# The first feed-forward product in seven block products for eight, on one NeuronCore

## The chip, the core and the metric

The kernel runs on one NeuronCore of a Trainium2 chip. The metric is device microseconds of one launch, from the first instruction to the end of the last store. The five engines are TensorE (PE in the profile, its weight loads PEld), VectorE (DVE), ScalarE (ACT), GpSimd (POOL) and SyncE (SP, here the queue that issues nearly all DMAs). Each engine runs its own instructions strictly in the order in which the program wrote them, and waits on semaphores that others raise. So an instruction that waits holds up everything behind it on its engine.

## What is computed

A transformer layer on x of 8 batches of 512 tokens and 512 features: cross attention with 16 heads, then a feed-forward part with a routed low-rank addition. The change is about the second part:

```
def _L0_ffn_ref(x, W1, W2, ln_g, ln_b, router_W, router_b, raw_U, raw_V, gamma):
    r_raw = _layernorm(x_flat, ln_g, ln_b) @ router_W.T + router_b
    r = jnp.clip(r_raw, -TAU, TAU)
    alpha = jax.nn.softplus(r)
    phi, idx = jax.lax.top_k(alpha, TOP_K)
    S_sum = jnp.sum(phi, axis=-1, keepdims=True)
    Z = phi / (S_sum + EPS) * jnp.tanh(S_sum)
    h_lat = jnp.einsum('nd,nkd->nk', x_flat, U_sel)
    dyn = jnp.einsum('nk,nkd->nd', h_lat * Z, V_sel).reshape(B, S, D) * gamma
    static = (jax.nn.gelu(x_flat @ W1.T, approximate=False) @ W2.T).reshape(B, S, D)
    return static + dyn
x = x + _L0_xattn_ref(_layernorm(x, axis=-1), ctx, ctx, mask, bias, ...)
x = x + _L0_ffn_ref(_layernorm(x, axis=-1), ...)
```

W1 is 2048 by 512, W2 is 512 by 2048, the router has 256 rows, and 8 of them are chosen per token.

## The kernel before

Three stages run one after the other, each a function: `project` (to about 290 us: the q, k and v products, and W1 and W2 split and stored for later), `attend` (to 853 us), and `blend` (to the end at 1799 us). The change is nearly all in `blend`.

**Precision.** A product of two float32 matrices is computed as three products of rounded halves (PASSES, high by high, high by low, low by high; type fp32r). The halves come from a copy to the high half and a subtraction for the low half. `project` stores both halves of W1 and W2 in `wf_d`, and `blend` loads them as pieces of 512 KB for each batch again (`load_w1`, `load_w2`, four slots each).

**The feed-forward loop.** A batch is 16 blocks f of 128 hidden features. `up(b, p, f)` makes one block for the batch's 512 tokens: 12 matmuls of 512 columns at L1695 (4 chunks of the inner dimension by 3 passes) that take W1's block as the stationary operand and the normalised tokens `zT` as the moving one. ScalarE applies the gelu (L1574), VectorE casts the high half `g_h` (L1463), GpSimd subtracts for the low half `g_l` (L1281). `down(b, f)` adds the block into the output, 12 matmuls at L1716, and is placed two blocks behind its `up` (LAG = 2). `ps_h` is two PSUM banks that `up` fills in turn.

**The rest of a batch** is spread over the same loop by block number: the output projection of the next batch's attention (`project_out`, 48 matmuls at L1618, blocks 6 and 7), the residual and the statistics on VectorE (`residual`, L1310 and L1313), normalisation and turning of the next tokens (block 8 and 9, L1327, L1612), routing of the next batch (`route`, blocks 10 to 12), softplus on ScalarE (`soften`, L1552 to L1557), choice and weights on VectorE (`choose`, `weigh`, `gains`, L1358 to L1397), then `turn_h` and `latent`. The tokens `zT` are held twice, so that all of this for batch b+1 runs beside batch b. All orders are written out by hand in each engine's `body`; no scheduler moves anything.

## Time and profile before

| | us |
|---|---|
| three runs, median (lowest to highest) | 1801.02 (1800.64 to 1802.78) |
| span of the profiled execution | 1799.0 |
| one batch in steady state (1064.13 to 1181.06) | 116.93 |
| TensorE busy in it | 116.93 |
| VectorE, ScalarE, GpSimd busy in it | 40.46, 24.32, 30.29 |

The profiled execution spans 1799.0 us from its first to its last instruction; the median of the runs is 2.0 us above that, which is what lies around the span and the scatter of the runs together. In a row of the trace's timeline the first number is the start in us from the span's beginning, the second the duration, then engine, line, operation, output and inputs with their shapes, and in brackets the idle time before it and who ended it. A matmul's duration overlaps with its neighbours', so the distance between two starts is what one costs.

### The profile page before, as it was taken

The page shows a single profiled execution, that of the slowest core. Times are in us where ns is not written, and L with a number is a line of the kernel's source. Part 1 is how long each engine was busy: PE and PEld are TensorE (multiplying, and loading weights), DVE is VectorE, ACT ScalarE, POOL GpSimd, SP SyncE. Part 2 cuts the span into 40 slices and gives each one's busy share as a digit, 9 for nine tenths or more (in the row PEclk, how much of TensorE's full clock was granted, in tenths as well). Part 3 has the DMA queues.
Part 4 walks back from the last instruction along what each step waited for, and adds up shares of the span by engine and source line. Part 5 has one row for each costly group of instructions (what it writes and reads, how often), then busy time and mean ns, then how long its engine had stood idle before and what let it go on. Part 6 is the DMA issues. An engine that isn't in the chain of part 4 may idle for free.

```text
span 1799.0 us, 29674 instructions
## 1 busy us (share of the span) xinstructions
PE 1784.4 (99%) x10800; PEld 1335.5 (74%) x10800; DVE 1041.7 (58%) x2438; ACT 813.8 (45%) x1819; POOL 832.9 (46%) x368
## 2 busy tenths in 40 slices
PE   9999999999999999999999999999999999999999
PEld 7888886555555555555788888888888888888887
DVE  7565558999999999998852324333342242332411
ACT  4322226999999999998232113122131131311300
POOL 1212128999999999996221232222312223223222
PEclk9999999999999999999999999999999999999999
DMA  9998999536346335420543645535546355464453
GB/s 327 338 358 291 343 337 363 191 110 221 97 140 202 128 126 203 138 93 19 201 153 116 213 157 175 188 117 189 191 143 226 128 188 170 138 217 154 152 188 128
DMA packets 198160, 339.98 MB, mean 189 GB/s; under 512 B 10625, under 2 KB 52225, under 8 KB 197505
## 3 DMA queue, kind: packets, MB, share of 16 engines
q1 hardware_dynamic: 194464, 324.98, 53.4%
q0 software_dynamic: 3264, 12.58, 1.9%
q8 instruction: 88, 1.44, 0.3%
q10 hardware_dynamic: 288, 0.52, 0.1%
q14 instruction: 56, 0.45, 0.1%
HBM read 268.84 MB, written 69.21 MB: 188 GB/s over the span
## 4 chain that ended last, share of the span: by engine, by line
PE 51%; DVE 1%; POOL 0%; issue 0%; ACT 0%; DVEq 0%; POOLq 0%; ACTq 0%
PE banks L1695 19%; PE banks L1716 19%; PE banks L1618 11%; PE banks L1612 1%; DVE k_x L1310 0%; DVE k_x L1455 0%; DVE n_aT_l L1302 0%; DVE n_zT_l L1302 0%; DVE n_stats L1313 0%; POOL n_rstd L1262 0%; POOL k_x L1256 0%; DVE h_k L1403 0%; POOL n_rs L1271 0%; DVE h_q L1421 0%; PE banks L1681 0%
## 5 line engine op out<-in xcount | busy, mean ns | idle before, releaser
L1281 POOL TENSOR_TENSOR n_g_l<-h_pos,n_g_h 128x512 fp32r<-128x512 f32 x128 | 175.1, 1368 | 601.9 <-DVE n_g_h L1463 601.9
L1716 PE MATMUL banks<-n_w,n_g_h 128*128 128x512 f32 x1024 | 316.7, 391 | 0.0
L1574 ACT ACTIVATE h_pos<-banks 128x512 f32<-128x512 f32 x128 | 75.5, 596 | 512.2 <-PE banks L1695 512.1
L1695 PE MATMUL banks<-n_zT_h,n_w 128*128 128x512 f32 x896 | 297.1, 390 | 0.0
L1463 DVE CAST n_g_h<-h_pos 128x512 fp32r<-128x512 f32 x128 | 54.4, 427 | 378.1 <-ACT h_pos L1574 378.1
L1063 ACT ACTIVATE l_tiles<-l_tiles,l_small 128x512 f32<-128x512 f32 x376 | 267.4, 715 | 0.1
L997 DVE CUSTOM_DVE_ANT_0 l_tiles<-banks,l_tiles 128x512 f32<-128x512 f32 x353 | 224.8, 687 | 25.8 <-PE banks L899 24.6
L910 PEld LDWEIGHTS banks<-ident,l_tiles 128*128 128x128 f32 x1524 | 163.3, 141 | 90.1 <-issue 70.5
L1716 PEld LDWEIGHTS banks<-n_w,n_g_h 128*128 128x128 f32 x1024 | 191.2, 188 | 39.3 <-POOL n_g_l L1281 0.4
L910 PE MATMUL banks<-ident,l_tiles 128*128 128x128 f32 x1524 | 207.5, 279 | 1.0 <-ACT a_pT L1041 0.9
L1716 PE MATMUL banks<-n_w,n_g_l 128*128 128x512 f32 x512 | 199.5, 390 | 0.0
L1695 PEld LDWEIGHTS banks<-n_zT_h,n_w 128*128 128x128 f32 x896 | 168.2, 188 | 34.7
L1695 PE MATMUL banks<-n_zT_l,n_w 128*128 128x512 f32 x448 | 174.4, 389 | 0.0
L1004 DVE COPY a_pT<-banks 128x512 f32<-128x512 f32 x256 | 164.5, 683 | 4.0 <-PE banks L910 3.1
L1041 ACT ACTIVATE a_pT<-banks 128x512 f32<-128x512 f32 x256 | 151.4, 592 | 29.1 <-PE banks L910 24.9
L924 PE MATMUL banks<-a_pT,a_v 128*32 128x256 f32 x2048 | 149.9, 388 | 0.0
L899 PE MATMUL banks<-h_k,h_q 32*128 32x512 f32 x1008 | 143.7, 639 | 2.4 <-PEq L158 0.5
L864 POOL TENSOR_TENSOR l_tiles<-a_pos,l_bias 128x2048 f32<-128x2048 f32 (+1 forms) x32 | 137.2, 4299 | 3.6 <-PE banks L910 3.3
L1716 PEld LDWEIGHTS banks<-n_w,n_g_l 128*128 128x128 f32 x512 | 96.1, 188 | 20.1
L406 POOL TENSOR_TENSOR p_wf_l<-l_pos,p_wf_h 128x2048 fp32r<-128x2048 f32 x8 | 36.9, 4615 | 141.8 <-ACT p_wf_h L562 141.8
L1695 PEld LDWEIGHTS banks<-n_zT_l,n_w 128*128 128x128 f32 x448 | 84.2, 188 | 17.3
L1063 ACT ACTIVATE a_t_s<-a_t_s,l_small 128x512 f32<-128x512 f32 x128 | 91.5, 719 | 0.0
(230 smaller groups left out, 3199.5 us busy)
## 6 DMA issues: line engine op xcount, KB each, us to landing
n_w<-wf_d SPq DMA_DIRECT2D x256, 512.0 KB, 4.2
a_pos<-pos_d SPq DMA_DIRECT2D x16, 1024.0 KB, 5.6
l_bias<-in_bias POOLq DMA_DIRECT2D x9, 1024.0 KB, 8.3
l_tiles<-in_x SPq DMA_DIRECT2D x8, 1024.0 KB, 10.6
l_bias<-in_mask SPq DMA_DIRECT2D x8, 1024.0 KB, 14.2
k_d<-l_tiles SPq DMA_DIRECT2D x8, 1024.0 KB, 12.8
pos_d<-l_bias SPq DMA_DIRECT2D x8, 1024.0 KB, 12.2
v_d<-p_v_s SPq DMA_DIRECT2D x32, 256.0 KB, 7.0
```

The lines of the kernel that those rows point to most:

```text
L864: pool.tensor_tensor(out=t_s[j % NN][:, first:end, :], in0=pos_rows(b, qt, qt + 1).broadcast_to([P, end - first, S]), in1=bias_rows(first, ...
L899: pe.matmul(ps_s[:, i, :], q[rows, b, qt * P:(qt + 1) * P], k[rows, b, :], start=True, stop=True).then_inc(scored, 1)
L910: last = pe.transpose(ps_t[:, BANK[i], kt * P:(kt + 1) * P], t_s[at[1] % NN][:, i, kt * P:(kt + 1) * P], ident[:, :])
L924: last = pe.matmul(ps_o[rows, :], v[:, b, kt, rows], pT[:, h, i, kt, :], start=kt == 0, stop=kt == NT - 1)
L997: dve.tensor_tensor_reduce(t_s[j % NN][:, i:i + 1, :], ps_s[:, i:i + 1, :], added, 1.0, 3.0e38, ALU.add, ALU.min, nmax[:, j % NN, i:i + 1] ...
L1004: dve.tensor_copy(dst, src).then_inc(kept_dve, 1)
L1041: act.activation(dst, src, ACT.Copy).then_inc(kept_act, 1)
L1063: act.activation(t_s[j % NN][:, i, :], t_s[j % NN][:, i, :], ACT.Exp, scale=-1.0, bias=nmax[:, j % NN, i:i + 1], accum_out=total[:, j // 2 ...
L1281: pool.tensor_tensor(out=g_l[:, f % NG, :], in0=g_f[:, f % NG, :], in1=g_h[:, f % NG, :].bitcast(F32), op=ALU.subtract).then_inc(g_low, 1)
L1618: last = pe.matmul(dst, stationary, moving, start=start and n == 0, stop=stop and n == len(passes) - 1)
L1695: last = pe.matmul(ps_h[:, f % 2, :], stationary, moving, start=i == 0, stop=i == len(passes) - 1)
L1716: last = pe.matmul(ps_y[:, t, :], gs[i], w2[:, f % NW, j, :], start=f == 0 and m == 0, stop=f == NF - 1 and m == 2)
```

## The change

The product of W1 and the tokens is cut into two by two blocks: W1 into two halves of its hidden features and two of its inner dimension, the tokens into two halves of the inner dimension and two of the tokens. With sums of blocks on both sides, seven block products give what eight give (the scheme with 7 products and 15 additions). A batch is 8 units, each with the pair of 128-feature blocks f and f + 8. A unit has the products P1, P6, P2, P7, P5, P4 and P3, in this order on TensorE (`product`, L1848). Each is 6 matmuls of 256 columns (2 chunks by 3 passes, L1871), and so a batch has 336 matmuls of 256 columns for 192 of 512 columns. `down` is kept: 12 matmuls of 512 columns per block, now in four pieces `down(j, t)` of 3, spread between the products.

- **The results are put together from PSUM.** ScalarE copies P1 (`c1`, L1739). VectorE adds `u2` = P6 + c1 and `u3` = P7 + c1, then C22 = bank + u3, C21 = bank + c1 and C12 = bank + u2. P2 is added in PSUM to P1, P7 and P4 to P6, and P3 to P5, and a product that lands in a bank waits until the one before was read. The gelu takes three instructions per unit instead of two.
- **The tokens' sums.** `z_copies` take the turned tokens from PSUM, `z_sums` makes four sums on VectorE, `z_highs` and `z_lows` split the blocks, `z_sum_lows` on GpSimd splits the sums. The result `zo` is held once, not twice. Therefore the first unit of a batch (f = 0) has a seam on TensorE: the 8 pieces of `down` that are due, the last two turns and `latent` stand ahead of the new batch's first product.
- **W1's sums** are made in `project` by GpSimd (`weight_sums`), and seven operands per unit are stored in place of W1 and W2. In `blend` 448 loads of 256 KB fetch them into 9 slots.
- **W2** is loaded raw, 128 loads of 256 KB, and split again for each batch: `weight_high` on ScalarE (L1721), `weight_low` on GpSimd (L1356), two of each per unit.
- **The small work is placed anew.** Routing is of the batch itself, in its units 0 and 1; softplus is in unit 2, cut in two (`soften` ahead of the gelus of the unit, `soften_more` behind them), the weights in units 3 and 4, `turn_h` in unit 5, the next batch's `project_out` and `residual` in units 6 and 7. In batch 0 routing comes one unit later. `split(3, ...)` of `vg`, which before stood behind two casts, now stands ahead of the first unit on VectorE.
- Several semaphores are merged into one with a running count.

The core of the diff (removed loops stand in the functions above):

```diff
-    wf_d = nc.dram_tensor("wf_d", (NF, P, 4, D), F32, kind="Internal").ap()
+    wf_d = nc.dram_tensor("wf_d", (NF // 2, P, NP, 2, S // 2), F32, kind="Internal").ap()
...
+            def weight_low(j):
+                pool.wait_ge(w2_high, j + 1)
+                pool.tensor_tensor(out=w2[:, j % NG, 1, :], in0=w2_raw[:, j % 2, :], in1=w2[:, j % NG, 0, :].bitcast(F32),
+                                   op=ALU.subtract).then_inc(w2_low, 1)
...
+                gelu_low(2 * n - 1)
+                if f == UNITS - 1 and more:
+                    roots(b + 1)
+                weight_low(2 * n)
+                gelu_low(2 * n)
+                weight_low(2 * n + 1)
+                if f == 4 and more and b > 0:
+                    add_bo(b + 1, (b + 1) % 2)
...
+            split(3, vg[0][:, :, :], vg[1][:, :, :], lat_vg[:, :, :])
...
+            def behind_u2(b, f):
+                at, m = f - route_at(b), b + 1
+                if at in (0, 1):
+                    logits(b, 2 * at)
+                if f == 1 and b > 0:
+                    evacuate(b - 1, 0)
+                    evacuate(b - 1, 1)
+                if at == 2:
+                    clip(b)
+                    largest(b)
+                if at == 3:
+                    small_part(b)
+                if at == 4:
+                    weigh(b)
+                if f == UNITS - 1 and b < B - 1:
+                    if b > 0:
+                        residual(m, 3)
+                    moments(m)
+
+            def behind_u3(b, f):
+                at, m = f - route_at(b), b + 1
+                if f == 1 and b > 0:
+                    evacuate(b - 1, 2)
+                    evacuate(b - 1, 3)
+                if at in (0, 1):
+                    logits(b, 2 * at + 1)
+                if at == 2:
+                    choose(b)
+                if at == 3:
+                    large_part(b)
+                if at == 5:
+                    h_lows(b)
+                    if b < B - 1 and b > 0:
+                        att_low(m, (0, 1))
+                if f == 6 and b < B - 1 and b > 0:
+                    residual(m, 0)
+                if f == UNITS - 1 and b < B - 1:
+                    normalise(m)
+
+            def behind_c12(b, f):
+                at, m = f - route_at(b), b + 1
+                if at == 2:
+                    chosen(b)
+                if at == 3:
+                    alpha(b)
+                if at == 4:
+                    gains(b)
+                if at == 5 and b < B - 1 and b > 0:
+                    att_low(m, (2, 3))
+                if f == 6 and b < B - 1 and b > 0:
+                    residual(m, 1)
+                    residual(m, 2)
...
+                if f == 0 and b > 0:
+                    z_sums(b, 0)
+                    z_lows(b, 0)
+                    z_sums(b, 1)
+                    z_lows(b, 1)
+                dve.wait_ge(made, NP * n + P6 + 1)
+                dve.wait_ge(c1_done, n + 1)
+                dve.tensor_tensor(out=u2, in0=y_bank, in1=c1, op=ALU.add).then_inc(posted, 1)
+                gelu_high(2 * n - 1)
+                behind_u2(b, f)
+                dve.wait_ge(made, NP * n + P7 + 1)
+                dve.tensor_tensor(out=u3, in0=y_bank, in1=c1, op=ALU.add).then_inc(posted, 1)
+                behind_u3(b, f)
+                dve.wait_ge(made, NP * n + P5 + 1)
+                dve.wait_ge(posted, NPOST * n + U3)
+                need(dve, g_low, 2 * n - NG + 1)
+                dve.tensor_tensor(out=row_1[:, HALF:S], in0=x_bank, in1=u3, op=ALU.add).then_inc(posted, 1)
+                dve.wait_ge(made, NP * n + P4 + 1)
+                dve.tensor_tensor(out=row_1[:, 0:HALF], in0=y_bank, in1=c1, op=ALU.add).then_inc(posted, 1)
+                dve.wait_ge(made, NP * n + P3 + 1)
+                need(dve, g_low, 2 * n + 1 - NG + 1)
+                dve.tensor_tensor(out=row_0[:, HALF:S], in0=x_bank, in1=u2, op=ALU.add).then_inc(posted, 1)
+                gelu_high(2 * n)
+                behind_c12(b, f)
...
+                act.wait_ge(made, NP * n + P1 + 1)
+                act.activation(c1, ps_h[:, n % 2, 0:HALF], ACT.Copy).then_inc(c1_done, 1)
+                if at in (0, 1):
+                    keep_lat(b, 2 * at)
+                act.wait_ge(made, NP * n + P2 + 1)
+                need(act, g_low, 2 * n + 1 - NG + 1)
+                act.activation(g_f[:, (2 * n + 1) % NG, 0:HALF], ps_h[:, n % 2, 0:HALF], ACT.Gelu).then_inc(gelu_done, 1)
+                weight_high(2 * n)
+                if at in (0, 1):
+                    keep_lat(b, 2 * at + 1)
+                if at == 2:
+                    soften(b)
+                if at == 4:
+                    bound(b)
+                if at == 5:
+                    h_highs(b)
+                    if b < B - 1 and b > 0:
...
+                act.wait_ge(posted, NPOST * n + C21)
+                act.activation(g_f[:, 2 * n % NG, :], g_f[:, 2 * n % NG, :], ACT.Gelu).then_inc(gelu_done, 1)
+                act.wait_ge(posted, NPOST * n + C12)
+                act.activation(g_f[:, (2 * n + 1) % NG, HALF:S], g_f[:, (2 * n + 1) % NG, HALF:S], ACT.Gelu) \
+                    .then_inc(gelu_done, 1)
+                weight_high(2 * n + 1)
+                if at == 2:
+                    soften_more(b)
...
+            def product(n, i):
+
+                b, f = n // UNITS, n % UNITS
+                if i == P1:
+                    need(pe, posted, NPOST * (n - 1) + C21)
+                    if f == 0:
+                        pe.wait_ge(zb_low, 2 * b + 2)
+                elif i == P6:
+                    need(pe, posted, NPOST * n)
+                    if f == 0:
+                        pe.wait_ge(zs_low, 2 * b + 2)
+                elif i == P2:
+                    pe.wait_ge(c1_done, n + 1)
+                elif i == P5:
+                    pe.wait_ge(gelu_done, NGELU * n + G11)
+                else:
+                    pe.wait_ge(posted, NPOST * n + {P7: U2, P4: U3, P3: C22}[i])
+                q = NP * n + i
+                pe.wait_ge(w1_in[q % NR], 16 * (q // NR + 1))
+                bank = ps_h[:, (n + (i in (P6, P7, P4))) % 2, 0:HALF]
+                passes = [(w1[:, q % NR, m, k * P:(k + 1) * P], zo[:, j, MOVING[i], k, :])
+                          for k in range(2) for m, j in PASSES]
+                for s, (stationary, moving) in enumerate(passes):
+                    last = pe.matmul(bank, stationary, moving, start=s == 0 and i in (P1, P6, P5),
+                                     stop=s == len(passes) - 1, skip_group_check=True)
+                last.then_inc(made, 1)
...
+            def behind_product(b, f, i):
+                at, m = f - route_at(b), b + 1
+                if at in (0, 1) and i in (P6, P7):
+                    route(b, 2 * at + (i == P7))
+                if at == 5 and i == P6:
+                    turn_h(b, 0)
+                    turn_h(b, 1)
+                if f == 6 and m > 1 and m < B and i in (P6, P7, P4, P3):
+                    project_out(m, (P6, P7, P4, P3).index(i))
+                if f == UNITS - 1 and m < B and i == P3:
+                    turn_z(m, TURNS[0])
+                    turn_z(m, TURNS[1])
+                if f == UNITS - 1 and m == B and i == P6:
+                    latent(b)
+
+            def unit(b, f):
+                n = UNITS * b + f
+                early, late = 2 * n - 3, 2 * n - 2
+                seam = f == 0 and b > 0
+                if seam:
+                    for t in range(NT):
+                        down(early, t)
+                    turn_z(b, TURNS[2])
+                    turn_z(b, TURNS[3])
+                    for t in range(NT):
+                        down(late, t)
+                    latent(b - 1)
+                for i in range(NP):
+                    product(n, i)
+                    behind_product(b, f, i)
+                    if i % 2 and not seam:
+                        down((early, late)[i == P4], 2 * (i == P7))
+                        down((early, late)[i == P4], 2 * (i == P7) + 1)
+                if not seam:
+                    down(late, 2)
+                    down(late, 3)
```

**ScalarE, softplus of the first batch.** `n_ln_w`, `n_u`, `h_k` and `h_bias` are its tiles, `h_pos` the gelu's, `h_bias` also `c1` after the change. Before:

```order
L1552 ACTIVATE h_k<-h_q 128x1024 [waits n_clip_done]
L1554 ACT_TABLE_LOAD
L1554 ACTIVATE h_k<-h_k 128x1024 [waits n_abs_done]
L1556 ACTIVATE h_bias<-h_k 128x1024 [waits n_u_done]
L1557 ACT_TABLE_LOAD
L1557 ACTIVATE h_bias<-h_k 128x1024
L1574 ACT_TABLE_LOAD [waits n_g_low]
L1574 ACTIVATE h_pos<-banks 128x512 [waits n_hidden]
```

After:

```order
L1705 ACTIVATE n_u<-h_q 128x1024 [waits n_chosen_of]
L1707 ACT_TABLE_LOAD
L1707 ACTIVATE n_u<-n_u 128x1024 [waits n_softened]
L1757 ACT_TABLE_LOAD
L1757 ACTIVATE h_pos<-h_pos 128x512 [waits n_posted]
L1759 ACTIVATE h_pos<-h_pos 128x256 [waits n_posted]
L1721 ACTIVATE n_w<-h_bias 128x512 [waits n_g_used,h_w2_in1]
L1711 ACTIVATE n_w<-n_u 128x1024 [waits n_softened]
L1712 ACT_TABLE_LOAD
L1712 ACTIVATE n_ln_w<-n_u 128x1024
L1739 ACTIVATE h_bias<-banks 128x256 [waits n_made]
L1744 ACT_TABLE_LOAD [waits n_g_low]
```

The gelus stand in the middle of the softplus, with one more table load, and the copy `c1` of the next unit stands behind all of it.

**VectorE, the residual of a batch to come.** `k_x` is the residual, `n_o_ready` is raised by `project_out`. Before:

```order
L1310 TENSOR_TENSOR k_x<-banks,k_x 128x512 [waits n_o_ready,k_xb_done]
L1313 BN_STATS n_stats<-k_x 128x6 [waits n_o_read]
L1310 TENSOR_TENSOR k_x<-banks,k_x 128x512 [waits n_o_ready,k_xb_done]
L1313 BN_STATS n_stats<-k_x 128x6 [waits n_o_read]
```

After:

```order
L1654 TENSOR_TENSOR h_pos<-banks,h_bias 128x256 [waits n_g_low,n_made]
L1574 CAST n_g_h<-h_pos 128x512 [waits n_g_used,n_gelu_done]
L1400 TENSOR_TENSOR k_x<-banks,k_x 128x512 [waits n_o_ready,k_xb_done]
L1403 BN_STATS n_stats<-k_x 128x6 [waits n_o_read]
L1400 TENSOR_TENSOR k_x<-banks,k_x 128x512 [waits n_o_ready,k_xb_done]
L1403 BN_STATS n_stats<-k_x 128x6 [waits n_o_read]
```

The second residual is now behind C12 (L1654), which waits for P3. On TensorE `project_out` stood behind the 12 matmuls of a `down`, before:

```order
L1716 MATMUL banks<-n_w,n_g_h 128x512 x2
L1716 MATMUL banks<-n_w,n_g_l 128x512
L1716 MATMUL banks<-n_w,n_g_h 128x512 x2
L1716 MATMUL banks<-n_w,n_g_l 128x512
L1618 MATMUL banks<-k_wo_h,n_aT_h 128x512 [waits n_o_read]
```

and now, with P3 in the first two rows:

```order
L1894 MATMUL banks<-n_w,n_g_h 128x512 x2
L1894 MATMUL banks<-n_w,n_g_l 128x512
L1871 MATMUL banks<-n_zo,n_w 128x256 [waits h_w1_in0,n_posted]
L1871 MATMUL banks<-n_zo,n_w 128x256 x5
L1778 MATMUL banks<-k_wo_h,n_aT_h 128x512 [waits n_o_read]
```

The fourth `project_out`, which waits for the second residual's read, stands directly behind P3.

**VectorE at the start of `blend`.** `n_ru` and `n_vg` are the router's and the low-rank part's halves. Before:

```order
L1332 TENSOR_TENSOR n_zT_l<-banks,n_zT_h 128x512 [waits n_t_high] x4
L1439 TENSOR_TENSOR h_q<-h_q,h_pos 128x256 [waits n_g_mean_done]
L1439 TENSOR_TENSOR h_q<-h_q,h_pos 128x256 x3
```

and, further on, behind two residuals and the router's splits:

```order
L1295 TENSOR_TENSOR n_ru_l<-banks,n_ru_h 128x2x256 [waits n_w_high]
L1463 CAST n_g_h<-h_pos 128x512 [waits n_gelu_done] x2
L1293 CAST n_vg_h<-h_bias 128x1024
L1295 TENSOR_TENSOR n_vg_l<-h_bias,n_vg_h 128x1024 [waits n_w_high]
L1463 CAST n_g_h<-h_pos 128x512 [waits n_gelu_done]
```

After:

```order
L1426 TENSOR_TENSOR h_k<-h_k 128x2x256 [waits n_z_copied]
L1429 TENSOR_TENSOR h_k<-h_k 128x256 [waits n_zs_done]
L1431 TENSOR_TENSOR h_k<-h_k 128x256 [waits n_zs_done]
L1426 TENSOR_TENSOR k_az<-k_az 128x2x256 [waits n_z_copied]
L1429 TENSOR_TENSOR k_az<-k_az 128x256 [waits n_zs_done]
L1431 TENSOR_TENSOR k_az<-k_az 128x256 [waits n_zs_done]
L1435 TENSOR_TENSOR n_zo<-h_k,n_zo 128x4x256 [waits n_zb_high]
L1435 TENSOR_TENSOR n_zo<-k_az,n_zo 128x4x256 [waits n_zb_high]
L1553 TENSOR_TENSOR h_q<-h_q,h_pos 128x256 [waits n_g_mean_done]
L1553 TENSOR_TENSOR h_q<-h_q,h_pos 128x256 x3
```

and further on, behind the same residuals and splits:

```order
L1386 TENSOR_TENSOR n_ru_l<-banks,n_ru_h 128x2x256 [waits n_w_high]
L1384 CAST n_vg_h<-n_w 128x1024
L1386 TENSOR_TENSOR n_vg_l<-n_w,n_vg_h 128x1024 [waits n_w_high]
L1640 TENSOR_TENSOR h_bias<-banks,h_bias 128x256 [waits n_c1_done,n_made]
L1644 TENSOR_TENSOR h_bias<-banks,h_bias 128x256 [waits n_made]
```

The last two rows are `u2` and `u3` of the first unit; all above them is the stage's set-up.

## Rows read from the trace of the kernel before

**Rows 1.** The page's first part: busy us, share of the span and instructions.
```profile
PE 1784.4 (99%) x10800; PEld 1335.5 (74%) x10800; DVE 1041.7 (58%) x2438; ACT 813.8 (45%) x1819; POOL 832.9 (46%) x368
```
**Rows 2.** The chain of work that ended last, by line.
```profile
by line: PE banks L1695 19.4%; PE banks L1716 19.3%; PE banks L1618 11.2%; PE banks L1612 1.1%; issue 0.2%; DVE k_x L1310 0.2%; DVE k_x L1455 0.2%; DVE n_aT_l L1302 0.1%; DVE n_zT_l L1302 0.1%; DVE n_stats L1313 0.1%; POOL n_rstd L1262 0.1%
```
**Rows 3.** Batch and stage: PE, PEld, DVE, ACT, POOL busy, granted clock, DMA share.
```profile
1064.13:1181.06 116.93, 116.93 (x529) 97.11 (x528) 40.46 (x83) 24.32 (x38) 30.29 (x25) 1.00 0.51 171
853.00:1799.00 946.00, 940.26 (x4243) 779.35 (x4242) 337.61 (x701) 197.20 (x306) 236.86 (x197) 1.00 0.51 168
```
**Rows 4.** Timeline of one block's chain, all engines.
```profile
1071.13 0.39 PE L1695 MATMUL banks<-n_zT_h,n_w 128*128 128x512 f32 x1
...
1071.56 0.60 ACT L1574 ACTIVATE h_pos<-banks 128x512 f32<-128x512 f32 x1 [2.10 <-PE banks L1695]
...
1072.19 0.43 DVE L1463 CAST n_g_h<-h_pos 128x512 fp32r<-128x512 f32 x1 [1.90 <-ACT h_pos L1574]
...
1072.70 1.28 POOL L1281 TENSOR_TENSOR n_g_l<-h_pos,n_g_h 128x512 fp32r<-128x512 f32 x1 [5.93 <-DVE n_g_h L1463]
```
**Rows 5.** TensorE and its weight loads: a piece of the chain, and the timeline.
```profile
876.93 5.74 PE banks L1618 x24
...
874.56 1.97 PE L1612 MATMUL banks<-ident,k_az 128*128 128x128 f32 x16 [1.28 <-DVE k_az L1327]
876.93 0.50 PE L1618 MATMUL banks<-k_wo_h,n_aT_h 128*128 128x512 f32 x1 [0.41 <-DVE k_x L1310]
...
876.93 0.19 PEld L1618 LDWEIGHTS banks<-k_wo_h,n_aT_h 128*128 128x128 f32 x1 [0.64 <-DVE k_x L1310]
877.04 0.19 PEld L1618 LDWEIGHTS banks<-k_wo_l,n_aT_h 128*128 128x128 f32 x1
```
**Rows 6.** Groups of instructions of one batch: count, busy us, mean ns, idle before.
```profile
L1544 ACT ACTIVATE n_aT_h<-k_az 128x512 fp32r<-128x512 f32 x4 | 2.2, 622 | 0.0
L1548 ACT ACTIVATE h_q<-banks 128x256 f32<-128x256 f32 x4 | 1.5, 384 | 15.8 <-DVE h_q L1347 15.8
L1554 ACT ACT_TABLE_LOAD x1 | 1.3, 1283 | 0.0
L1554 ACT ACTIVATE h_k<-h_k 128x1024 f32<-128x1024 f32 x1 | 1.1, 1062 | 0.0
...
L1374 DVE SCALAR_TENSOR_TENSOR h_bias<-h_q,h_bias 128x1024 f32<-128x1024 f32 x1 | 2.2, 2198 | 0.0
L1383 DVE CUSTOM_DVE_ANT_0 h_k<-h_bias,h_k 128x256 f32<-128x256 f32 x4 | 1.5, 422 | 0.2 <-DVE h_bias L1378 0.2
```
**Rows 7.** Timeline of `gains`, and the shortest, median and longest of its kind.
```profile
1111.41 1.29 POOL L1281 TENSOR_TENSOR n_g_l<-h_pos,n_g_h 128x512 fp32r<-128x512 f32 x1 [5.29 <-DVE n_g_h L1463]
1111.44 2.73 DVE L1397 SCALAR_TENSOR_TENSOR h_q<-h_k,n_coef,h_q 128x256 f32<-128x256 f32 x4
...
L1397 DVE SCALAR_TENSOR_TENSOR h_q<-h_k,n_coef,h_q x32: 470/472/1548, 928.5 to 1698.4; 128x256 f32<-128x256 f32 x32
```
**Rows 8.** Timeline of the start of `blend`: VectorE, and the first `up`.
```profile
879.16 0.41 DVE L1434 TENSOR_TENSOR n_r_row<-banks,n_r_row 128x256 f32<-128x256 f32 x1
879.50 2.47 DVE L1332 TENSOR_TENSOR n_zT_l<-banks,n_zT_h 128x512 fp32r<-128x512 f32 x4
881.89 1.42 DVE L1439 TENSOR_TENSOR h_q<-h_q,h_pos 128x256 f32<-128x256 f32 x4
883.23 0.68 DVE L1310 TENSOR_TENSOR k_x<-banks,k_x 128x512 f32<-128x512 f32 x1
...
886.58 1.23 DVE L1295 TENSOR_TENSOR n_ru_l<-h_q,n_ru_h 128x1024 fp32r<-128x1024 f32 x1
...
891.04 1.78 DVE L1293 CAST n_vg_h<-h_bias 128x1024 fp32r<-128x1024 f32 x1
892.86 2.19 DVE L1295 TENSOR_TENSOR n_vg_l<-h_bias,n_vg_h 128x1024 fp32r<-128x1024 f32 x1
...
883.30 0.48 PE L1695 MATMUL banks<-n_zT_h,n_w 128*128 128x512 f32 x1
```

743 lines of the change are left out of this document (358 added, 385 removed).

## The prediction

> **What bounds the kernel now.** I read the page's busy times first: TensorE is busy 99% of the span, the next engine 58% [rows 1]. The chain of work that ended last is TensorE's by line, with the two products of the feed-forward part, L1695 and L1716, at the top [rows 2]. The windows say it of one batch: 116.93 us long, TensorE busy 116.93 of it, the granted clock 1.00, which is the 2.4 GHz level [rows 3]. So in `blend` nothing waits but TensorE's own queue. What takes matmul time away is gained in full, and every wait that TensorE gets is lost in full. VectorE has 76 us of a batch free, ScalarE 92, GpSimd 87; load alone makes none of them the bound. The question is whether, in order, they answer TensorE in time.
>
> **Part 1, the matmuls.** One 512-column matmul costs the distance between two starts. 24 of them take 5.74 us [rows 5]; less the last one's 0.39 and 0.11 of start-up that is 5.24 / 23 = 0.228 us. Removed are 192 a batch, 1536 in all, 349.9 us. Added are 336 a batch, 2688 of 256 columns, which the trace does not have. Strassen's arithmetic gives 7/8, but only if half the columns cost half the time. Bounds: after an idle stretch the second weight load starts 0.11 us after the first, and the first matmul takes 0.50 for 0.39, again 0.11 more [rows 5], so a load needs 0.11 and cannot be outrun: 2688 x 0.110 = 295.7, a gain of 54.2. On the other side 512 columns at 2.4 GHz are 0.213, and if the remaining 0.0145 belongs to the matmul and not to its columns, 256 cost 0.107 + 0.0145 = 0.121: 325.2, a gain of 24.7. The 16 transposes, each with a load of its own, run (1.97 - 0.27) / 15 = 0.113 apart [rows 5] (0.27 being an estimate of the last one's own length). That is the nearest row, but of another type, so I go a little above it: 0.115, 309.1 us, a gain of **40.8 us**. If the whole 0.19 of a load were exposed, the change would cost 161 us (a rival).
>
> The rows show the load 0.11 and the 512-column distance 0.228. The Trainium skill, "TensorE: Matmul & The Clock Gate", sections "LDWEIGHTS (loading the stationary operand)" and "Back-to-back issue gap", gives columns / 1.2, 107 ns, for a load and N / 2.4 + 2.5 ns for a matmul, 109 ns at 256 columns. By it the gain is an estimate of 57 us and the total 16 us lower than mine. For 512 columns it says 216 ns where the trace has 228, so I don't follow it down.
>
> **Part 2, new waits in every unit.** Before, `up` had no link to another engine but a free bank; now a product needs an addition or a copy of the product before the last. Measured from the last matmul's turn, ScalarE starts 0.20 us later (1071.13 + 0.23 to 1071.56) [rows 4]; an addition from PSUM of 256 columns is 0.41 [rows 8], a copy 0.38 [rows 6]. With 0.05 to signal, a link needs 0.7. It has two pieces of `down`, 6 x 0.228 = 1.37, and a product, 6 x 0.115 = 0.69, so 2.06, or at the tightest the 0.69. So an ordinary unit is free of waits, as long as the answering engine is idle. Where small work is queued ahead of the link, it isn't. I walked the queues of a batch in order:
>
> - *Softplus on ScalarE, unit 2.* Count from the end of P6. The first gelu starts at 1.37 + 0.69 + 0.20 = 2.26. Then come, before the next unit's `c1`: gelu 0.38, weight 0.62, Abs 1.06, table 1.28, Exp 1.06, table 1.28, gelu 0.60, gelu 0.38, weight 0.62, Identity 1.06, table 1.28, Ln 1.06, and `c1` 0.38 [rows 4, 6]: 11.06, with gaps of 0.02 and the signal 11.4. `c1` is there at 13.7. The next P2 would go after 5 pairs of `down` and 7 products, 11.66. Wait 2.0 (1.6 to 2.4), each batch: **16.0**.
> - *`gains` on VectorE, unit 4.* C12 is done 0.61 after P3, the cast 0.43, the small product 0.15, the four `gains` 2.73, because the first of them runs beside GpSimd's subtraction and takes 1.55 for 0.47 [rows 7]. Now a second subtraction, W2's, stands right behind the first on GpSimd. `turn_h` is wanted 1.37 + 2 x 0.69 = 2.75 after P3, and gets them at 3.9 or more: 1.5 (0.5 without the overlap, 2.4 with two): **12.0**.
> - *`residual` on VectorE, unit 6, six batches.* The fourth `project_out` stands directly behind P3 and waits for the second residual: 0.20 + C12 0.41 + cast 0.43 + 0.68 [rows 4, 8], less what overlaps: 1.6 (1.1 to 1.9): **9.6**.
> - *Unit 3*: the large step of the weights takes 2.2 [rows 6] between U3 and C22; the slack is 0.3 where GpSimd leaves it alone, and a subtraction of 1.28 in front [rows 4] breaks it. 0.7 (0 to 1.6): **5.6**. *Unit 4*: four reductions of 0.42 and their small steps [rows 6], 2.4 in all, between U2 and U3: 0.45 (0 to 0.9): **3.6**. *The seam*: the token chain (copies, sums, splits) has 48 matmuls and 8 turns, 24 of the 48 being `latent`'s, as cover, some 12 to 14 us, and needs about as much: 0.2 (0 to 0.5): **1.6**.
>
> In all 48.4 us (27 to 74). Whether GpSimd's overlap falls on these steps decides half of the range. The row shows one overlap costing 1.08 us. The Trainium skill, "SBUF — State Buffer", section "🔬 SBUF: two separate sides", says that a VectorE instruction with two SBUF inputs and a GpSimd instruction hold a shared port in turn for the whole instruction. The trace agrees, with 1548 beside 472 ns. It speaks against this change, which doubles GpSimd's long subtractions; without any such overlap the waits would come to the 27 of the lower bound.
>
> **Part 3, the start of `blend`.** The first `up` started at 883.30 [rows 8] and the next three followed beside VectorE's set-up. Now `u2` stands behind all of it. VectorE is through with its row at 879.5. Six sums (two of 512 and four of 256 elements, by 0.68 and 0.41) are 3.0, the lows 2 x 1.23; then centring 1.42, two residuals 2 x 1.3, splits 0.7 + 1.2 + 4 x 0.68, and `vg`'s 0.7 + 1.2 if alone or 1.78 + 2.19 as in the trace [rows 8]. That ends at 895.5 to 900. TensorE has until then P1, P6 and P2, 2.1 us, for 883.3 onwards: 10 to 14.6 us idle; nothing else is at hand, since the first `down` and routing come later. What was beside it before is not needed twice, so I allow 8 to 15: **12.5**.
>
> **Part 4, no cost.** `project` stores fewer bytes and GpSimd gets four small sums a batch; TensorE there has its own work, 0 (-2 to 2). The raw load of W2 and 448 loads of 256 KB are issued 9 slots ahead, and the DMA share is 0.51 [rows 3]: covered. If that cover failed, each product would wait for its landing, over 1 us each; nothing in the share speaks for it. GpSimd goes from 30 to some 55 us of a batch: free. The end: 36 matmuls of `down` for 24, but the last unit's own work is taken from the same total.
>
> **The sum.** 1799.0 - 40.8 + 48.4 + 12.5 = 1819.1 of span, and the median lies 2.0 above the span: **1821 us**, slower by 1.1%.
>
> **Rivals.**
> - *The waits are small and the matmuls cheap*, 0.22. 0.111 a matmul gains 51.5. GpSimd never meets VectorE's steps: softplus 1.8 x 8, `gains` 0.6 x 8, residual 1.3 x 6, nothing else, 27. The start costs 8. 1799.0 - 51.5 + 27 + 8 + 2 = **1785**. It decides as soon as waits and start together stay below what the matmuls give back. For it: all links have 2.06 us, and other engines are idle more than half; against it the softplus queue, which no such luck shortens.
> - *About unchanged*, 0.08: the pace of 0.111 with waits of about 43 and the start at 8, **1800**.
> - *The overlap always falls badly*, 0.15: 0.119 a matmul (gain 30), waits 70, start 15: **1856**. GpSimd has four long subtractions a unit, so a VectorE step of 2 us mostly meets one.
> - *The load is not hidden*, 0.05: this is slower by one mechanism, TensorE's weight path. Each 256-column matmul costs 0.19, 510.7 in all, +160.8. The products' windows grow and swallow softplus and most of `gains`, leaving some 25 of waits and start: **1987**. It decides from 0.130 a matmul on (349.9 / 2688), where the first gain is nil. Against it: the loads 0.11 apart.
> - *The change doesn't save what it says*, because W2's split on ScalarE and GpSimd becomes late for `down`: `down` is two or three blocks behind, some 14 us, and the split needs 0.62 + 1.3. No chance of its own.
>
> **How the numbers follow.** The forecast has 0.50. A measurement can tell 0.2%, 3.6 us, from no change, so 1797.4 to 1804.6 is "same". Faster is the first rival and the forecast's low end, 0.25; same 0.09; slower 0.66. The range, 1785 to 1856, reaches from the first rival to the third; outside remain the exposed load and the outer parts of both.
>
> **What the changed profile would show.** Part 1: starts of L1871 0.115 apart within a product (0.110 to 0.121), against 0.13 for nothing gained and 0.19 for the exposed load. Softplus: TensorE idle about 2 us before a P2 once a batch, released by ScalarE L1739. `gains`: idle before the L1842 turns, released by L1507 on VectorE, which would last some 2.7 us or more. Residual: idle before L1778 directly behind L1871. Start: `u2` (L1640) first at 895 or later, and TensorE nearly empty from 886. A batch would take 116.9 - 43.7 + 38.6 + 6 = 117.8 us for 116.93. I am wrong if the batch comes out under 114, which the waits would have to explain, or over 121.

## The result and the profile after

| | before | after |
|---|---|---|
| median of the runs, us | 1801.01 | 1876.41 (1874.95 to 1877.47) |
| profiled span, us | 1799.0 | 1873.1 |
| ratio | | 1.0415, 95% interval 1.0401 to 1.0430 |

The change makes the kernel 4.2% slower. I had forecast 1821 us, slower by 1.1%, with 1785 to 1856 as the range: the direction held, the size did not. The measured time lies 20 us above the range.

The page's first part and the granted clock, against [rows 1]:

```profile
span 1873.1 us, 34304 instructions
PE 1788.3 (95%) x11952; PEld 1382.7 (74%) x11952; DVE 1264.8 (68%) x2790; ACT 963.2 (51%) x2139; POOL 1102.6 (59%) x568
PEclk9999999999999999999899999999999999999999
```

TensorE is busy as long as before, 1788 us for 1784, and idle 85 us for 15. GpSimd grew from 833 to 1103 us, VectorE from 1042 to 1265. The clock has one slice below 9 tenths, that of 889.7 to 936.6 us, in which the first products stand.

One batch, from the transposes of `turn_h` (L1772) to those of the next batch, and the first 4 us of it. The columns are those of [rows 3]:

```profile
1204.10:1328.60 124.50, 117.05 (x672) 102.68 (x673) 68.30 (x128) 42.72 (x75) 59.76 (x44) 0.99 0.56 178
1204.10:1208.10 4.00, 4.00 (x17) 3.64 (x18) 1.36 (x2) 0.00 (x0) 3.73 (x3) 0.64 0.00 0
```

A batch takes 124.50 us for 116.93, and it has 7.45 us in which TensorE is idle. That is over the 121 us which I had named as the sign that I am wrong. What TensorE waited for, with the total in us, how often, and the longest:

```profile
PE banks L1772 <- DVE h_q L1507: 27.2, 8, 3.9
PE banks L1871 <- DVE h_bias L1644: 9.7, 8, 1.2
PE banks L1778 <- DVE k_x L1400: 9.1, 7, 1.4
PE banks L1871 <- ACT h_bias L1739: 7.0, 8, 0.9
PE banks L1871 <- DVE h_bias L1640: 6.5, 1, 6.5
PE banks L1871 <- issue: 6.0, 1, 6.0
PE banks L620 <- DVE p_fac_diag L528: 3.5, 1, 3.5
```

So there are four kinds of wait in a batch: `turn_h` for `gains` (3.9 in six batches, 1.9 in the first and the last), P4 of unit 4 for u3 behind `weigh` (1.2), the fourth `project_out` for the residual (1.4, in six batches), and P2 of unit 3 for `c1` (0.9). Two waits stand at the start of `blend`, one in `project`. In batch 2 ("..." stands for rows left out):

```profile
1110.21 0.50 PE L1778 MATMUL banks<-k_wo_h,n_aT_h 128*128 128x512 f32 x1 [1.45 <-DVE k_x L1400]
1110.55 0.40 PE L1778 MATMUL banks<-k_wo_l,n_aT_h 128*128 128x512 f32 x1
...
1111.95 0.39 PE L1778 MATMUL banks<-k_wo_l,n_aT_h 128*128 128x512 f32 x1
...
1178.73 1.45 PE L1871 MATMUL banks<-n_zo,n_w 128*128 128x256 f32 x10 [0.88 <-ACT h_bias L1739]
...
1189.39 1.59 PE L1871 MATMUL banks<-n_zo,n_w 128*128 128x256 f32 x12
...
1194.30 0.98 PE L1871 MATMUL banks<-n_zo,n_w 128*128 128x256 f32 x6 [1.22 <-DVE h_bias L1644]
...
1204.10 1.97 PE L1772 MATMUL banks<-ident,h_q 128*128 128x128 f32 x8 [3.90 <-DVE h_q L1507]
1205.72 1.20 PE L1894 MATMUL banks<-n_w,n_g_h 128*128 128x512 f32 x2
...
1207.08 0.62 PE L1894 MATMUL banks<-n_w,n_g_h 128*128 128x512 f32 x2
```

Two things stand here beside the waits. Twelve matmuls of 256 columns (two products) start within 1.59 - 0.28 = 1.31 us, 0.119 apart. And behind the long wait two `down` matmuls take 1.20 us, the same two 0.62 a little later. The granted clock is 0.64 in those 4 us, so it had fallen from its 2.4 GHz level to 1.2 for a part of them, behind an idle stretch of 3.9 us. TensorE is busy in all of the 4.00 us, so this costs 4.00 x (1 - 0.64) = 1.4 us on top of the wait. The same happens in seven of the eight batches (0.66 in the 4 us from 1079.45, 0.57 from 978.14 behind a wait of only 1.9), and not in the last (1.00 from 1824.92, also behind 1.9).

VectorE and GpSimd ahead of that wait, against [rows 7]:

```profile
1198.26 1.29 POOL L1351 TENSOR_TENSOR n_g_l<-h_pos,n_g_h 128x512 fp32r<-128x512 f32 x1 [5.38 <-DVE n_g_h L1574]
1198.29 5.76 DVE L1507 SCALAR_TENSOR_TENSOR h_q<-n_sel,n_coef,h_q 128x256 f32<-128x256 f32 x4
1199.51 1.45 POOL L1356 TENSOR_TENSOR n_w<-h_bias,n_w 128x512 fp32r<-128x512 f32 x1
...
1200.92 5.66 POOL L1325 TENSOR_TENSOR k_x<-k_x,k_bo_r 128x512 f32<-128x512 f32 x4
```

The four steps of `gains` take 5.76 us, and 1.67 where GpSimd is idle (e1 below). GpSimd runs a gelu subtraction, a W2 subtraction and then four additions of the output bias (`add_bo`), and VectorE gets its turn once between two of them. The four reductions of `weigh`, earlier in the same unit (all 32 of the kernel in the first row), and the cast ahead of them show the same:

```profile
L1493 DVE CUSTOM_DVE_ANT_0 n_sel<-n_w,n_sel x32: 411/956/1509, 965.9 to 1815.9; 128x256 f32<-128x256 f32 x32
...
1188.55 1.42 DVE L1574 CAST n_g_h<-h_pos 128x512 fp32r<-128x512 f32 x1
```

A reduction takes between 0.41 and 1.51 us. The cast has a single SBUF input, and it too takes 1.42 us for 0.42 where a GpSimd subtraction has just begun (1188.40).

The start of `blend`:

```profile
889.10 3.38 DVE L1435 TENSOR_TENSOR n_zo<-h_k,n_zo 128x1024 fp32r<-128x1024 f32 x1
892.41 3.35 DVE L1435 TENSOR_TENSOR n_zo<-k_az,n_zo 128x1024 fp32r<-128x1024 f32 x1
...
906.04 0.41 DVE L1640 TENSOR_TENSOR h_bias<-banks,h_bias 128x256 f32<-128x256 f32 x1
...
895.87 4.12 PE L1871 MATMUL banks<-n_zo,n_w 128*128 128x256 f32 x18 [6.01 <-issue]
906.51 6.18 PE L1871 MATMUL banks<-n_zo,n_w 128*128 128x256 f32 x36 [6.51 <-DVE h_bias L1640]
```

TensorE is idle 6.0 us ahead of P1 and 6.5 ahead of P7. The first wait is put down to "issue", but P1 waits for VectorE's second low, which ends at 892.41 + 3.35 = 895.76. The 18 matmuls of P1, P6 and P2 between the two waits are 0.21 apart, at half the clock (0.52 granted in these 4.12 us), and the first 15 of the next 36 are as slow (0.71 in their 6.18 us). The turns of batch 0's tokens start at 880.85, 6.3 us later than in [rows 5], so the first two stages became longer as well. Nearly all of it is in `project`: the last batch's first q product starts at 279.24 us for 274.63, and its first six matmuls run at half the clock behind the wait of 3.5 us (0.50 granted from 279.24 to 281.94).

### The profile page after: what moved, and what is told of

Its sections match the earlier page's. It is cut to its first block and busy times, and to the rows that moved or that the text cites. A ratio compares the mean times of both kernels' runs of the same rounds, so it can differ in the third digit from the quotient of the medians.

```text
span 1873.1 us, 34304 instructions
## 1 busy us (share of the span) xinstructions
PE 1788.3 (95%) x11952; PEld 1382.7 (74%) x11952; DVE 1264.8 (68%) x2790; ACT 963.2 (51%) x2139; POOL 1102.6 (59%) x568
## 5 line engine op out<-in xcount | busy, mean ns | idle before, releaser
L1351 POOL TENSOR_TENSOR n_g_l<-h_pos,n_g_h 128x512 fp32r<-128x512 f32 x128 | 193.5, 1512 | 378.5 <-DVE n_g_h L1574 378.5
L1871 PEld LDWEIGHTS banks<-n_zo,n_w 128*128 128x128 f32 x2688 | 359.8, 193 | 54.1 <-DVE h_bias L1644 11.4
L1871 PE MATMUL banks<-n_zo,n_w 128*128 128x256 f32 x2688 | 368.6, 286 | 29.3 <-DVE h_bias L1644 9.7
L1894 PE MATMUL banks<-n_w,n_g_h 128*128 128x512 f32 x1024 | 326.1, 400 | 0.0
L1356 POOL TENSOR_TENSOR n_w<-h_bias,n_w 128x512 fp32r<-128x512 f32 x128 | 180.1, 1407 | 89.6 <-ACT n_w L1721 89.6
L1894 PEld LDWEIGHTS banks<-n_w,n_g_h 128*128 128x128 f32 x1024 | 182.6, 192 | 28.4
L1744 ACT ACTIVATE h_pos<-banks 128x256 f32<-128x256 f32 x64 | 24.6, 385 | 173.4 <-PE banks L1871 173.3
L1757 ACT ACTIVATE h_pos<-h_pos 128x512 f32<-128x512 f32 x64 | 40.6, 634 | 136.0 <-DVE h_pos L1651 135.9
L1640 DVE TENSOR_TENSOR h_bias<-banks,h_bias 128x256 f32<-128x256 f32 x64 | 27.0, 422 | 118.4 <-PE banks L1871 86.7
L1654 DVE TENSOR_TENSOR h_pos<-banks,h_bias 128x256 f32<-128x256 f32 x64 | 27.2, 425 | 107.1 <-PE banks L1871 107.1
```

The costliest lines, as they stand in the source:

```text
L1351: pool.tensor_tensor(out=g_l[:, j % NG, :], in0=g_f[:, j % NG, :], in1=g_h[:, j % NG, :].bitcast(F32), op=ALU.subtract).then_inc(g_low, 1)
L1356: pool.tensor_tensor(out=w2[:, j % NG, 1, :], in0=w2_raw[:, j % 2, :], in1=w2[:, j % NG, 0, :].bitcast(F32), op=ALU.subtract).then_inc(w2_ ...
L1871: last = pe.matmul(bank, stationary, moving, start=s == 0 and i in (P1, P6, P5), stop=s == len(passes) - 1, skip_group_check=True)
L1894: last = pe.matmul(ps_y[:, t, :], gs[i], w2[:, j % NG, k, :], start=f == 0 and m == 0, stop=f == NF - 1 and m == 2)
```

## The experiments

My theory from this profile: one mechanism stands behind most of the waiting, namely that VectorE's instructions with two SBUF inputs and GpSimd's long instructions exclude one another. The rest of the waiting is queue order, and the product's pace is a matter of the matmul itself. The rival: VectorE and GpSimd are simply too full for four links a unit.

### What a 256-column matmul costs

**e4**, the kernel before with every `up` matmul in two halves:

```diff
-                for i, (stationary, moving) in enumerate(passes):
-                    last = pe.matmul(ps_h[:, f % 2, :], stationary, moving, ...)
+                for h in range(2):
+                    for i, (stationary, moving) in enumerate(passes):
+                        last = pe.matmul(ps_h[:, f % 2, h * 256:h * 256 + 256], stationary,
+                                         moving[:, h * 256:h * 256 + 256], ...)
```

> The kernel before with each up matmul of 512 columns done as two of 256, no block products, no new links. Theory (a 256-column fp32r matmul costs 0.1205 us whatever stands around it): 3072 x 0.1205 = 370 us for 349.9, and the 512-column ones behind them 5 ns slower each (some 6 us): 1801 + 20 + 6 = about 1827 us. Rival (the 0.1205 comes from the new loads, from DMA traffic or from the links, and half the columns cost half): within 5 us of 1801.

Measured 1823.12 us, ratio 1.0124 (1.0107 to 1.0141) to the kernel before, as all ratios here. A part of the timeline of one `up`:

```profile
1060.34 0.40 PE L1696 MATMUL banks<-n_zT_h,n_w 128*128 128x256 f32 x2
...
1062.13 0.28 PE L1696 MATMUL banks<-n_zT_h,n_w 128*128 128x256 f32 x1
```

From 1060.34 to 1062.13 are 15 distances between starts, 0.119 on average. Nothing of the block products is in this kernel, so the pace belongs to the 256 columns. Two halves cost 0.240 for 0.227 whole.

**e5**, the kernel before with each `up` matmul on 384 columns, the last 128 left out:

```diff
-                    last = pe.matmul(ps_h[:, f % 2, :], stationary, moving, ...)
+                    last = pe.matmul(ps_h[:, f % 2, 0:384], stationary, moving[:, 0:384], ...)
```

> The kernel before with each up matmul on 384 of its 512 columns; the last 128 are left out, so the output isn't the reference's. It tells what the 0.120 us of 256 columns is made of. If a fixed part of 14 ns comes with every matmul: 384 / 2.4 = 160 + 14 = 174 ns, 1536 x 0.174 = 267 us, 1801 - 350 + 267 = 1718 us. If the part grows with the columns (227 / 512 x 384 = 170 ns), and 256 columns are slow only because the weight loads cannot follow: 261.5 us and 1713 us. The distance between two starts in the trace decides, 174 or 170.

```profile
1066.51 0.51 PE L1695 MATMUL banks<-n_zT_h,n_w 128*128 128x384 f32 x2
1066.85 0.33 PE L1695 MATMUL banks<-n_zT_l,n_w 128*128 128x384 f32 x1
1067.03 0.33 PE L1695 MATMUL banks<-n_zT_h,n_w 128*128 128x384 f32 x1
```

Three distances in 0.52 us, 0.173 each, at the end of an `up`; the first six of an `up` are slower, up to 0.185. Measured are 0.120, 0.173 and 0.227 us for 256, 384 and 512 columns, so 128 more columns cost 0.053 or 0.054 each time, which is one column per cycle of 2.4 GHz. By that the columns are 0.107, 0.160 and 0.213 us, and what is left is 0.013 to 0.014 each time: a fixed part per matmul. The time, 1734.46 us, is 16 us above the expectation. The slower first six are some 3 of it, and waits for the gelu's bank, 3.4 us, are another part; the rest I have not traced.

### Who holds up `gains` and `weigh`

**e1**, `gains` ahead of C12, where GpSimd is idle for 5 us:

```diff
-                if at == 4:
-                    gains(b)
...
+                if f - route_at(b) == 4:
+                    gains(b)
                 dve.wait_ge(made, NP * n + P3 + 1)
```

> The four steps of gains on VectorE are moved from behind C12 to ahead of it, where GpSimd stands idle. Theory (a VectorE step with two SBUF inputs and a GpSimd subtraction exclude one another, so gains is held up by whatever GpSimd runs behind the cast): the four take 1.9 us instead of 5.76, the transposes behind P6 of unit 5 no longer wait (4.06 us in six batches, 2.05 in two), TensorE's clock doesn't fall behind that wait (about 0.8 us a batch); C12 comes some 0.2 us later, which nobody sees. 1876.4 - 28.5 - 5 = about 1843 us. Rival (gains is slow by itself after the change, by its new tiles or by VectorE's load): the four still take over 2.7 us and then hold up C12 as well, 1870 to 1885 us.

Measured 1839.76 us, ratio 1.0216 (1.0201 to 1.0232), 36.7 us less than the changed kernel.

```profile
L1507 DVE SCALAR_TENSOR_TENSOR h_q<-n_sel,n_coef,h_q x32: 476/480/485, 971.2 to 1786.7; 128x256 f32<-128x256 f32 x32
```

The three numbers behind x32 are the shortest, the median and the longest in ns: all 32 steps take 0.48 us, where the changed kernel has 473/1484/1544. The four take 1.67 us, and the wait before `turn_h` is gone. The gain is 9.5 us more than the 27.2 of the waits, and the half clock behind seven of them, some 1.4 us each, is 10: the clock now stays at 1.00 there.

**e2**, only `add_bo` one unit later (`if f == 5` for `if f == 4` on GpSimd):

> Only the four additions of the output bias on GpSimd (add_bo) go one unit later. Theory of exclusion: gains in batches 1 to 6 meets two GpSimd instructions, not three or four, and takes about 3.7 us as in the two batches without add_bo; the wait falls from 4.06 to 2.05 in six batches and some of the lost clock comes back: 1876.4 - 12 - 3 = about 1861 us, unless the additions now meet the steps of unit 5 and 6 (0 to 8 us given back). Rival (the wait comes from the tanh or the cast ahead of gains): unchanged, 1876 us.

Measured 1863.80 us, ratio 1.0350 (1.0334 to 1.0365). 

```profile
L1507 DVE SCALAR_TENSOR_TENSOR h_q<-n_sel,n_coef,h_q x32: 471/980/1548, 973.5 to 1812.1; 128x256 f32<-128x256 f32 x32
```

and in TensorE's list of waits:

```profile
PE banks L1772 <- DVE h_q L1507: 15.1, 8, 1.9
```

With two GpSimd instructions beside them instead of three or four, the steps' median falls to 980 ns and the wait to 1.9 us in every batch. The dose follows the theory. My expectation had some of the lost clock coming back as well, and that it did not. Behind a wait of 1.9 us, in the 4 us from 1199.29, the columns being those of [rows 3]:

```profile
1199.29:1203.29 4.00, 4.00 (x15) 3.48 (x16) 0.62 (x2) 0.00 (x0) 1.27 (x1) 0.57 0.29 96
```

The granted clock is 0.57, and it fell behind all eight waits. The gain, 12.6 us, is the 12.1 us of idle time.

**e3**, GpSimd's subtractions on 16 columns for 512, and `add_bo` later:

```diff
-                pool.tensor_tensor(out=w2[:, j % NG, 1, :], in0=w2_raw[:, j % 2, :], ...)
+                e = D if j < NG else 16
+                pool.tensor_tensor(out=w2[:, j % NG, 1, 0:e], in0=w2_raw[:, j % 2, 0:e], ...)
```

and the same for the gelu's low half. The rest of the low halves is left out.

> GpSimd's two kinds of subtraction (low halves of the gelu and of W2) run on 16 columns for 512 from the fifth on, and add_bo one unit later; the rest of the low halves is left out, so the output isn't the reference's. Theory of exclusion: with GpSimd nearly idle every VectorE step has its own length; the waits before P4 of unit 4 (1.37 us) and before the transposes (4.06) are gone, those for c1 (1.04) and the residual (1.61) stay: 1876.4 - 11 - 28.5 - 5 = about 1832 us, matmuls still 0.120 to 0.121 us apart. Rival (VectorE is simply overloaded, 56 of 100 us): the waits stay.

Measured 1824.26 us (two runs), 8 us under the expectation. Of the steady waits only those for `c1` and for the residual are left, as expected, and the steps of `gains` have their own length:

```profile
L1509 DVE SCALAR_TENSOR_TENSOR h_q<-n_sel,n_coef,h_q x32: 480/481/485, 973.1 to 1773.9; 128x256 f32<-128x256 f32 x32
PE banks L1780 <- DVE k_x L1402: 9.1, 7, 1.5
PE banks L1873 <- ACT h_bias L1741: 7.0, 8, 0.9
```

`gains` and `weigh` stand where they stood, VectorE has the same instructions to do, and they don't hold anybody up once GpSimd is short. So it is not VectorE's load.

**e8**, e1 with `weigh` in two pairs, two reductions behind u2 and two (with the small steps) between C22 and C21:

```diff
-                for t in range(NT):
+                for t in range(2):
                     dve.tensor_tensor_reduce(sel[:, t, :], w[:, t, :], sel[:, t, :], ...)
...
+                if f - route_at(b) == 4:
+                    weigh_more(b)
                 dve.wait_ge(made, NP * n + P4 + 1)
```

> On top of e1: the four reductions of weigh in two pairs, one behind u2 and one between C22 and C21, where GpSimd is idle. Theory of exclusion: the wait of 1.37 us before P4 of unit 4 goes in eight batches, 1839.8 - 11 = about 1829 us. Rival (the reductions and small steps are simply too long for their place): the wait moves to P1 of the next unit or to P6, 1836 us or more.

Measured 1832.36 us, 7.4 less than e1 for 11 expected. The wait for u3 is gone in all batches. But a new one of 1.2 us has come in six batches, before P3 of unit 5, where `att_low` meets `add_bo`:

```profile
1190.14 5.24 POOL L1325 TENSOR_TENSOR k_x<-k_x,k_bo_r 128x512 f32<-128x512 f32 x4
1194.52 3.10 DVE L1393 TENSOR_TENSOR n_aT_l<-k_az,n_aT_h 128x512 fp32r<-128x512 f32 x2
```

Two steps of 0.68 took 3.10 us. In e1 they took 2.42, and the wait before P3 was 0.6 us; the gain partly went into the next collision.

### The queue of ScalarE

In the changed kernel, from the weight copy of unit 2 to `c1` of unit 3:

```profile
1168.33 0.62 ACT L1721 ACTIVATE n_w<-h_bias 128x512 fp32r<-128x512 f32 x1
1168.85 1.05 ACT L1705 ACTIVATE n_u<-h_q 128x1024 f32<-128x1024 f32 x1
...
1178.32 0.37 ACT L1739 ACTIVATE h_bias<-banks 128x256 f32<-128x256 f32 x1
```

**e6**, the softplus in one piece ahead of unit 2's gelus (`soften_more(b)` directly behind `soften(b)`):

> ScalarE runs the softplus in one piece, ahead of the gelus of unit 2, so that one table load of 1.28 us goes. Theory (the copy c1 of the next unit is late by what stands ahead of it in ScalarE's queue): c1 comes 1.28 us earlier, the wait of 1.04 before P2 is gone in eight batches, 1876.4 - 8 = about 1868 us. Rival (the gelus, now up to 5 us later, hold up the cast on VectorE and with it the next additions, or the next down): the wait returns elsewhere, 1874 to 1885 us.

Measured 1885.67 us, 9 us slower than the changed kernel. My expectation had the count wrong. Between Abs and `c1` stand three table loads (rows ACT_TABLE_LOAD of 1.28 us, where the function changes, as from Exp to the gelu) in either order, and the one that goes was behind `c1`. The gelus came 3 us later:

```profile
1176.80 0.64 ACT L1758 ACTIVATE h_pos<-h_pos 128x512 f32<-128x512 f32 x1
...
1177.46 0.43 DVE L1574 CAST n_g_h<-h_pos 128x512 fp32r<-128x512 f32 x1 [3.60 <-ACT h_pos L1758]
...
1178.16 0.36 ACT L1739 ACTIVATE h_bias<-banks 128x256 f32<-128x256 f32 x1
```

`c1` starts at the same place, and on VectorE the cast waits 3.6 us and pushes what is behind it, up to u3 of unit 3: a second wait there, 0.6 us before P4. These waits are 5 of the 9 us; the rest I have not traced.

**e12**, the logarithm alone moved, into unit 3 behind the first gelu and weight copy:

```diff
+                act.wait_ge(softened, NSOFT * m + EXP_DONE)
+                act.activation(w[:, :, :], u[:, :, :], ACT.Identity, bias=1.0).then_inc(softened, 1)
             def soften_more(m):
...
+                if at == 3:
+                    soften_more(b)
...
-                if at == 2:
-                    soften_more(b)
```

> The changed kernel with one edit: the logarithm of the softplus goes into the next unit, behind its first gelu and weight copy, and the addition of one stays with the exponential. Ahead of c1 then stand 2.3 us less (a table load and the logarithm). Theory: the wait of 1.04 us before P2 goes in eight batches and nothing takes its place, since the gelus of unit 2 are where they were: 1876.4 - 8.3 = about 1868 us. Rival (as with the softplus in one piece, something else on VectorE is late next): 1873 us or more.

Measured 1868.47 us, ratio 1.0375, 7.9 us less. The wait for `c1` is gone and none has taken its place. So it is the queue ahead of `c1`, and not the number of table loads, which is 35 here as in the changed kernel.

### The first stage

**e7**, the last batch's `weight_sums` on GpSimd behind the mask tiles:

```diff
-                weight_sums(b)
                 if not more:
                     mask_tiles()
+                weight_sums(b)
```

> In project, the last batch's four sums of W1 on GpSimd go behind the two mask tiles instead of ahead. Theory (they wait for W1's load at 264.8 us and push the mask tiles of 4.6 us each over VectorE's diagonal, for which TensorE waits 3.5 us at 278.5): that wait goes and most of the 6.3 us that the first two stages became longer: 1876.4 - 3.5 to 6 = about 1871 us. Rival (the 6.3 us come from the stores and loads of W1's operands): unchanged, 1876 us.

Measured 1872.60 us as the median of runs from 1867.1 to 1877.6. The wait of 3.5 us for L528 is gone, and the profiled span is 1867.8 for 1873.1. The runs scatter more than the gain, which the median puts at 4 us, so the times alone don't show it; the trace does. One part of the scatter is in the traces. Where `attend` begins TensorE waits for its own sequencer (PEq L162), 1.2 us in the changed kernel, 2.1 here, and 0.5 to 3.5 in the other traces. What decides that I don't know.

### All at once, and the start

**e9** has e1, e2, e7, e8, e12 and the fourth `project_out` behind the unit's last pieces of `down` instead of directly behind P3.

> All causes found in the steady batches taken away at once: gains ahead of C12, add_bo a unit later, weigh in two pairs, the logarithm of the softplus one unit later (only Abs, Exp and the addition of one ahead of the gelus, so that a table load and the logarithm, 2.3 us, no longer stand ahead of c1), the fourth project_out behind the last pieces of down, the sums of W1 behind the mask tiles. Theory (each wait has its own cause in an in-order queue): from 1876.4 go 28.5 + 5 (gains and clock), 11 (weigh), 8.3 (c1), 8 (residual), 5 (project): about 1811 us, no wait over 0.3 us left between units of batches 2 to 7, batch period 115 to 116 us. Rival (the waits stand in for one another, since VectorE and GpSimd are too full, as when the softplus was moved in one piece): new waits take their places, 1825 us or more.

Measured 1801.98 us, ratio 1.0009 (1.0000 to 1.0018), 9 us better than expected. My sum had 5 us for the clock where it is 10, and the collision that e8 had made is gone, since `add_bo` stands elsewhere. The window of one batch:

```profile
1088.95:1203.95 115.00, 114.94 (x672) 101.27 (x672) 63.59 (x128) 42.72 (x75) 59.62 (x44) 1.00 0.60 193
```

and the head of TensorE's list of waits:

```profile
PE banks L1878 <- DVE h_bias L1643: 6.5, 1, 6.5
PE banks L1878 <- issue: 6.0, 1, 6.0
```

Both stand at the start of `blend`; the third in the list is 1.5 us at the very beginning of the kernel. TensorE is busy for 114.94 of 115.00 us at full clock. The waits did not stand in for one another. A batch is 1.9 us shorter than before the change, which is what the seven products give: 43.8 - 336 x 0.120 = 3.5, less 1.6, which I put down to the slower 512-column matmuls (below).

**e10** spreads the set-up of `blend` over the first two units (residuals behind u2 and u3, the router's splits and `vg`'s later, routing one unit later).

> The kernel of e9, and the set-up on VectorE at the start of blend spread over the first two units of batch 0 (residuals behind u2 and u3, router's splits behind C12 of unit 0 and in unit 1, vg's split behind C12 of unit 1, routing of batch 0 in units 2 and 3). Theory (u2 of the first unit waits 6.5 us only for what is queued ahead of it): that wait goes, 2 to 3 us come back in the small gaps between the first products, and the clock, which fell to half in the idle stretch, comes back sooner: e9 minus 4 to 7 us, about 1805 us. Rival (TensorE has no other work there, so the same microseconds are waited for further on): within 1 us of e9.

Measured 1800.74 us, ratio 1.0000 (0.9991 to 1.0010). The 6.5 us wait is gone, waits of some 4 us in all have taken its place further on, and the 6.0 us ahead of P1 stayed. The difference to e9, 1.2 us, is within the scatter: nearer to the rival.

**e11** is e10 with the start turned around: sums and lows directly behind the normalisation, all of them on VectorE, two `project_out` behind P6 and P7.

> The kernel of e10 with the start of blend turned around: the tokens' sums and lows stand on VectorE directly behind the normalisation, GpSimd's two subtractions of 1024 elements (which held VectorE's lows at 3.4 us each for 1.2) are done by VectorE too, the first two residuals and the g_mean additions follow, and the two project_out of batch 1 that stood ahead of the first product stand behind P6 and P7 of unit 0. Theory (TensorE's first product waits 6 us for VectorE's and ScalarE's chain of sums and lows, of which 3 us are queue order and 2 to 4 the exclusion): the first product starts 4 to 6 us earlier by the sum of the work ahead of it, and the gaps among the first products are filled: e10 minus 4 to 8 us, about 1794 us. Rival (the same VectorE work merely stands behind instead of ahead, and the products wait there): within 2 us of e10.

Measured 1804.43 us, ratio 1.0021 (1.0012 to 1.0030): missed. One reason is that the sums had moved beside `add_bo` (879.72 to 885.29 on GpSimd) and met it:

```profile
881.20 1.55 DVE L1424 TENSOR_TENSOR h_k<-h_k 128x512 f32<-128x512 f32 x1 [1.21 <-ACT h_k L1690]
882.79 1.38 DVE L1427 TENSOR_TENSOR h_k<-h_k 128x256 f32<-128x256 f32 x1
```

against 0.96 and 0.42 in the changed kernel. Another is that the two `project_out` no longer stand ahead of P1 as cover, where TensorE still waits 5.8 us; the two are not told apart. The profiled run also had the longest wait at the head of `attend`, 3.5 us.

**e13** is e10 with one edit, GpSimd's two subtractions of 1024 elements on VectorE:

```diff
-            z_sum_lows(0, 0)
-            z_sum_lows(0, 1)
...
             z_lows(0, 1)
+            for k in range(2):
+                dve.wait_ge(zs_high, k + 1)
+                dve.tensor_tensor(out=zo[:, 1, T4:T3 + 1, k, :], in0=z_raw[k][:, T4:T3 + 1, :], ...)
```

> The kernel of e10 with one edit: GpSimd's two subtractions of 1024 elements at the start of blend are done by VectorE behind its own two lows; the order of e10 stays, so the additions of the output bias on GpSimd keep their old place ahead of the tokens' sums. Theory (VectorE's two lows take 3.4 us each for 1.2 only because they stand beside GpSimd's): the first product starts 4.3 us earlier; its successor waits for two more lows of 1.2 us each, so of VectorE's queue 6.7 us become 4.9 and the first u2 comes about 1.8 us earlier: e10 minus 2 us, about 1799 us. Rival (the lows are slow by themselves at 1024 elements in this layout): the four take 3.4 us each, and the start is 7 us longer, 1808 us.

```profile
885.55 1.22 DVE L1433 TENSOR_TENSOR n_zo<-h_k,n_zo 128x1024 fp32r<-128x1024 f32 x1
...
888.00 0.95 PE L1893 MATMUL banks<-n_zo,n_w 128*128 128x256 f32 x6 [1.72 <-issue]
```

The lows take 1.22 us for 3.38, and the wait ahead of P1 is 1.7 for 6.0, with a new one of 1.3 behind it for VectorE's last low. Measured 1797.58 us, ratio 0.9981 (0.9972 to 0.9990). More work on VectorE made the start shorter. This version leaves nothing of the computation out and is 0.2% faster than the kernel before.

## Why the prediction was wrong

**What bounds the kernel, right.** TensorE's queue is the bound, and each wait was lost in full. Also that load makes none of the others the bound: e3 and e9 show it.

**Part 1, the matmuls: mis-sized by 14 us.** I took 0.115 us, going by the transposes, and the trace has 0.120: 2688 x 0.120 = 323 us, a gain of 27 for the 41 that I summed. It is practically my upper bound (0.121), and the reason for that bound is the true one: 0.013 us come with every matmul (e4, e5). I chose the row of another type over the arithmetic on rows of the same type. The Trainium skill, "TensorE: Matmul & The Clock Gate", section "Back-to-back issue gap", would have given 109 ns and is further off: the fixed part it has is 2.5 ns, the runs show 13 with fp32r. Something I had no term for: the first six or so 512-column matmuls behind a run of products are 0.227 to 0.235 apart, 0.231 on average, where the kernel before has 0.227. The six behind P2 and P7 from 1188.01 to 1189.39 are an example. e4, without block products, has the same. Over the 240 of a batch that is about 1 us, and the batch window of e9 leaves 1.6 us that nothing else explains. I count some 10 us in all.

**Part 2, the waits.** I had named six places in a batch; four came true, and no seventh came up. The sizes:

| wait, us per batch | forecast | measured idle | what the runs say |
|---|---|---|---|
| `gains` | 1.5 (0.5 to 2.4) | 3.9 in six batches, 1.9 in two | e1, e2, e3 |
| half clock behind it | 0 | some 1.4 in seven batches | gone with the wait in e1 |
| softplus, `c1` | 2.0 (1.6 to 2.4) | 0.9 | e12 |
| residual | 1.6 | 1.4 | e9 |
| `weigh` | 0.45 (0 to 0.9) | 1.2 | e3, e8 |
| large step, unit 3 | 0.7 | 0 | none |
| seam | 0.2 | 0 | none |

The step that failed is the one on `gains`: 12.0 us forecast, 27.2 of idle time and some 10 of half clock in the trace, and 36.7 in e1. I had the mechanism (the first step takes 1.55 for 0.47 beside a GpSimd subtraction), but counted one or two such overlaps. I missed that `add_bo` with its four additions stands directly behind the second W2 subtraction of just this unit, so that each of the four steps waits for another GpSimd instruction: 5.76 us. The rule would have given the right price if I had walked GpSimd's queue as I did ScalarE's: as many overlaps as VectorE has steps, as long as GpSimd has work. The Trainium skill, "SBUF — State Buffer", section "🔬 SBUF: two separate sides", says that whichever of the two starts first holds the shared port for its whole instruction. The trace agrees, with 473 to 1544 ns for one and the same step in the changed kernel and 476 to 485 in e1. The same error made `weigh` nearly three times as long a wait as I had it.

Softplus was too dear mostly because I added durations; short ScalarE instructions follow one another closer than they last (weight copy 0.62, next start 0.52 later). From the gelu's start to the end of `c1` are 10.6 us for my 11.4, and the products being slower gave `c1` 0.3 more. The large step of unit 3 takes 1.99 us, near the 2.2 that I had, and TensorE doesn't wait for it; the slack is more than my 0.3.

The idle time of all these waits together is 52.6 us, and I had 48.4. That this sum is near is luck: `gains` and `weigh` are 21 us too cheap in it, softplus, unit 3, the seam and the residual 17 too dear. The half clock comes on top, and I had no term for it.

**Part 3, the start: right in its place, and 3 to 4 us short in its size.** 12.5 us were forecast; the trace has 6.0 + 6.5 of idle time, and some 33 matmuls at half the clock cost 3 to 4 more. The first u2, at 906.04, would without the 6.3 us of the earlier stages be at 899.7, in my 895.5 to 900. But I had put the wait ahead of P1 at nearly nothing. It came from the lows beside GpSimd, 3.4 us each for 1.23, the same mechanism once more (e13).

**Part 4, "no cost", wrong.** `project` and `attend` became 6.3 us longer; my bound was 2. The sums wait for W1's load in GpSimd's queue and push the mask tiles behind them, and TensorE waits 3.5 us (gone in e7) and then runs at half the clock for 2.7. DMA was covered, as forecast: no DMA is in TensorE's list of waits.

In sum, against the forecast of 74 less 20 = 54 us too few in the span: matmuls 14, the 512-column pace some 10, idle time of the waits 4, the half clock behind `gains` 10, the start 3 to 4, the first stages 6. That is 48; the remaining 6 us I cannot place from the rows, the slower first product behind each of the other waits (six matmuls in 0.98 for 0.88) being a part.

**The rivals.** The third, "the overlap always falls badly", at 0.15, was the nearest in mechanism and in time. Its 1856 was not low for its waits, which it had at 70 us where idle time and half clock together are 63. It lacked the 512-column pace and the longer first stages, and had 3 us too much of gain.

## What to carry to other kernels

A sum that counts on halved instructions needs the fixed part of an instruction first: 7/8 of the columns in twice as many matmuls gave 27 us of the 44 that 7/8 promises. Where two engines exclude one another, walk both queues: the price is not one overlap but one for every step, for as long as the other has work, and putting the step where the other is idle (e1), or even giving the other's work to the engine that waits (e13), takes that price away. A wait costs more than its idle time where the clock falls behind it: here 37 us for 27. When a change adds links to a tight queue, look at each small step that was harmless behind two blocks of slack; here six single moves brought 74 of 75 us back (e9).

## What the runs showed of the hardware

- An fp32r matmul, with a weight load of its own, costs its columns at 2.4 GHz and 0.013 us: 0.120, 0.173 and 0.227 us for 256, 384 and 512 columns (e4, e5, before).
- Behind a run of 256-column matmuls the next six or so of 512 columns are 0.231 apart on average, in the changed kernel and in e4, for 0.227.
- VectorE's steps with two SBUF inputs and GpSimd's instructions alternate one by one: four steps of 0.48 us took 1.67 us alone (e1) and 5.76 beside GpSimd, and the median of one was 480 ns in e1, 980 in e2 and 1484 in the changed kernel. A cast with one SBUF input was held too (1.42 us for 0.42). Where VectorE began first, GpSimd was held (a subtraction of 1.28 us took 2.20 at 1179.62, beside a step of VectorE from 1179.46). Additions with an input in PSUM kept their 0.42 us.
- After idle stretches of 3.9 us the granted clock was 0.64 to 0.66 over the next 4 us. After 1.9 us it fell as well in all eight batches of e2 (0.57 from 1199.29) and in one of two in the changed kernel. After the waits of 1.5 us and less it stayed at 1.00 (from 1110.21 and from 1194.30).
